# A graph network kernel on one core: four edits around edge preparation, the GCN projection and the first root's low parts

## The reference

```
L0  dense attention over an edge mask, 8 heads, then a feed-forward of 1024
L1  lin + PReLU, then twice: aggregate over edges, two 512x512 products, batch norm
L2  GCN: h = relu(layernorm(x)); aggregate(h / sqrt(deg)) @ W + b, leaky relu
L3  two relational layers: w[r] = sum_b att[r,b] * basis[b]   (30 bases of 512x512)
      out = x @ root + bias + sum_r A_r @ (gate_r * (x @ w[r]))
```

## Time and profile before

| | |
|---|---|
| median of 3 runs | 458.7 us (457.14 to 459.46) |
| profiled execution | 456.62 us, its span 454.8 us |
| TensorE busy | 438.6 us, 96% of the span |
| VectorE busy | 346.3 us, 76% |
| ScalarE busy | 243.7 us, 54% |
| GpSimd busy | 42.9 us, 9% |
| granted TensorE clock | 1.000 |
| DMA | 99.22 MB, mean 218 GB/s |

### The profile page before, as it was taken

The page is one execution under the profiler, slowest core; times in us unless marked ns, Lnnn a source line. Parts: engine busy times, 40 slices in busy tenths (PEclk is TensorE's granted clock), DMA queues, the critical chain, the costliest instruction groups (busy, mean ns, idle before and its releaser), DMA issues.

```text
span 454.8 us, 6200 instructions
## 1 busy us (share of the span) xinstructions
PE 438.6 (96%) x2226; PEld 274.3 (60%) x2226; DVE 346.3 (76%) x736; ACT 243.7 (54%) x428; POOL 42.9 (9%) x59
## 2 busy tenths in 40 slices
PE   8999999899997899999999999999998999999997
PEld 3334554443432346768776866677465788888885
DVE  5999996899999968688779657675759695866212
ACT  5999994676897617543345436544534623511210
POOL 3240000024223011000010000010000000000000
PEclk9999999999999999999999999999999999999999
DMA  7997347426699859978099766777973550000002
GB/s 254 415 398 176 110 174 308 179 93 219 235 380 353 295 206 332 409 272 345 11 372 404 295 246 251 275 252 267 375 199 115 225 186 1 1 0 2 0 3 92
DMA packets 18090, 99.22 MB, mean 218 GB/s; under 512 B 2959, under 2 KB 3599, under 8 KB 7567
## 3 DMA queue, kind: packets, MB, share of 16 engines
q1 hardware_dynamic: 13191, 72.72, 43.4%
q0 software_dynamic: 4000, 25.18, 15.1%
q10 hardware_dynamic: 864, 0.86, 0.6%
HBM read 93.50 MB, written 5.25 MB: 217 GB/s over the span
## 4 chain that ended last, share of the span: by engine, by line
PE 70%; DVE 12%; DMA 8%; issue 8%; ACT 1%; POOL 0%; DVEq 0%; POOLq 0%
PE bank L1371 15%; PE sbank L1703 10%; PE bank L1716 6%; PE sbank L1357 6%; PE sbank L1427 6%; PE bank L1608 5%; DMA bring<-in_basis 4%; PE bank L1688 4%; PE sbank L1567 3%; PE bank L1450 3%; DMA wring<-in_weights 3%; PE bank L1357 3%; PE bank L1513 2%; PE sbank L1337 2%; PE sbank L1490 2%
## 5 line engine op out<-in xcount | busy, mean ns | idle before, releaser
L839 DVE TENSOR_SCALAR cnt<-iota_row,edge_f 128x512 bf16<-128x512 f16 x132 | 41.4, 350 | 0.4 <-PE sbank L1427 0.4
L1357 PE MATMUL sbank<-bring,attw 120*32 120x512 f32 x336 | 41.0, 599 | 0.1
L1427 PE MATMUL sbank<-cnt,adjT 128*128 128x512 bf16 x132 | 30.6, 380 | 0.3
L466 ACT ACTIVATE stat<-stat,eps 128x1 f32<-128x1 f32 x32 | 9.4, 294 | 39.3 <-DVE stat L858 39.3
L576 ACT ACTIVATE adjT<-distance,edge_w,edge_f 128x128 bf16<-128x128 bf16 x61 | 29.2, 479 | 1.4 <-PE sbank L1427 1.4
L1281 DVE SCALAR_TENSOR_TENSOR y_lo<-sbank,gate,y_hi 128x512 fp32r<-128x512 f32 x16 | 11.8, 750 | 22.6 <-ACT y_hi L765 22.5
L497 ACT ACTIVATE s<-bank,colsb 128x512 f32<-128x512 f32 x24 | 16.4, 687 | 21.8 <-PE bank L1371 21.8
L1427 PEld LDWEIGHTS sbank<-cnt,adjT 128*128 128x128 bf16 x132 | 12.3, 98 | 21.7 <-DVE cnt L839 6.4
L529 ACT ACTIVATE distance<-iota_row,edge_f 128x128 bf16<-128x128 f16 x61 | 24.3, 400 | 1.8 <-DVE edge_f L905 0.4
L1371 PE MATMUL bank<-hT_hi,w_hi 128*128 128x512 f32 x64 | 25.3, 395 | 0.0
L1371 PE MATMUL bank<-hT_hi,w_lo 128*128 128x512 f32 x64 | 24.9, 390 | 0.0
(11 more groups left out here) (250 smaller groups left out, 1092.5 us busy)
## 6 DMA issues: line engine op xcount, KB each, us to landing
bring<-in_basis SPq DMA_DIRECT2D x59, 1024.0 KB, 9.8
wring<-in_weights POOLq DMA_DIRECT2D x8, 1024.0 KB, 10.0
landing<-in_weights POOLq DMA_DIRECT2D x4, 1024.0 KB, 5.1
w_scratch<-stage SPq DMA_DIRECT2D x16, 256.0 KB
hT<-in_weights POOLq DMA_DIRECT2D x4, 1024.0 KB, 9.1
qkw<-w_scratch POOLq DMA_DIRECT2D x2, 2048.0 KB, 7.9
rring<-in_rows POOLq DMA_DIRECT2D x12, 256.0 KB, 8.5
wring<-in_basis SPq DMA_DIRECT2D x2, 1024.0 KB, 12.9
```

The costliest lines, as they stand in the source:

```text
L839: dve.tensor_scalar(hot_s[:, n % HOT, :], iota[:, :], src_f[:, n:n + 1], None, ALU.is_equal).then_inc(sem("hot_ready"), 1)
L1357: mm = pe.matmul(unit_bank(b)[32 * j:32 * j + 32, :], attw[0:KB, u // UNITS, g, :], unit_place(u)[0:KB, j, :], start=(g == 0), stop=(g == ...
L1427: pe.matmul(bank[7][:, :], hot_d[:, n % HOT, :], hot_s[:, n % HOT, :], start=(n == 0), stop=(n == ECH - 1)).then_inc(sem("hot_used"), 1)
```

## The change

Five places are touched. (1) All four tiles of x are issued by SP; ACT's queue begins with `dst` and `src`, and `etype` counts on `cols_loaded`, which is now waited for at 48. (2) DVE prepares the destination's two parts, the source and the float of the destination ahead of the statistics of x; the relation, the field and the weight stay behind `hT0`. (3) The low parts of `root1` are written by POOL, behind its load and ahead of `load_w(0)`, and are gone from DVE. (4) `units(5)` and the four zero products become `units(6)`, so that every later unit of that stretch is one further on, and `units(2)` becomes `units(1)`. (5) The GCN projection runs in the order `BY_TILE`.

```
--- before.py
+++ after.py
@@ -318,7 +318,7 @@
             @block.sync
             def _(sp):
 
-                for c in (0, 2):
+                for c in range(C):
                     sp.dma_start(xr[:, c, :], x[:, c, :]).then_inc(sem(f"x{c}_loaded"), 16)
                 sp.dma_start(colsb[:, :], cols).then_inc(sem("cols_loaded"), 16)
                 sp.dma_start(alph[:, :], alphas.partition_broadcast(P)).then_inc(sem("cols_loaded"), 16)
@@ -402,6 +402,17 @@
                     pool.wait_ge(sem(last), C)
                     pool.dma_start(row(name), rows[i, :].partition_broadcast(P)).then_inc(
                         sem(f"row_slot{i % RSLOTS}_loaded"), 16)
+
+                def low_parts(name, ks=range(C)):
+
+                    hi, lo = weight_parts(name)
+                    i = IN_PARTS.index(name)
+                    for k in ks:
+                        pool.wait_ge(sem("weight_hi"), i * C + k + 1)
+                        if i and k == 0:
+                            pool.wait_ge(sem("weight_parts"), i * C)
+                        pool.tensor_tensor(lo[:, k, :], weight(name)[:, k, :], hi[:, k, :].bitcast(F32),
+                                           ALU.subtract).then_inc(sem("weight_parts"), 1)
 
                 def load_w(layer):
 
@@ -454,6 +465,7 @@
                     pool.dma_start(gate_rows[:, i, :], gate_scratch[i, :].partition_broadcast(P)).then_inc(
                         sem("gate_rows"), 16)
                 load_weight("root1")
+                low_parts("root1")
                 load_w(0)
                 load_weight("root2")
                 load_w(1)
@@ -531,10 +543,9 @@
 
 
                 my_chunks = [n for n in range(ECH) if on_act(n)]
-                for c in (1, 3):
-                    act.dma_start(xr[:, c, :], x[:, c, :]).then_inc(sem(f"x{c}_loaded"), 16)
-                for i, e in enumerate((src, dst, etype)):
+                for i, e in ((1, dst), (0, src)):
                     act.dma_start(edge_i[:, i, :], e).then_inc(sem("edges_loaded"), 16)
+                act.dma_start(edge_i[:, 2, :], etype).then_inc(sem("cols_loaded"), 16)
                 act.wait_ge(sem("small"), 1)
                 act.activation(root_of_eps[:, :], eps[:, :], ACT.Sqrt)
 
@@ -581,7 +592,7 @@
                     t, at = divmod(n - FIRST_TILE - TILE_LAG, TILE_EVERY)
                     if at == 0 and 0 <= t < 2 * C:
                         if t == 0:
-                            act.wait_ge(sem("cols_loaded"), 32)
+                            act.wait_ge(sem("cols_loaded"), 48)
                         qk_take(t)
                         if t == C + 1:
                             stage_units(BATCH)
@@ -874,6 +885,14 @@
                     dve.wait_ge(sem("v_psum"), c + 1)
                     dve.tensor_tensor(vr[:, c, :], bank[v_bank(c)][:, :], row("bv"), ALU.add).then_inc(sem("v"), 1)
 
+                dve.wait_ge(sem("edges_loaded"), 32)
+                dve.tensor_scalar(dst_part[:, 0, :], edge_i[:, 1, :], P - 1, None, ALU.bitwise_and).then_inc(
+                    sem("edge_step"), 1)
+                dve.tensor_scalar(dst_part[:, 1, :], edge_i[:, 1, :], P.bit_length() - 1, None,
+                                  ALU.logical_shift_right).then_inc(sem("edge_step"), 1)
+                dve.tensor_copy(src_f, edge_i[:, 0, :]).then_inc(sem("edge_step"), 1)
+                dve.wait_ge(sem("edge_step"), 3)
+                dve.tensor_copy(dst_lo, dst_part[:, 0, :]).then_inc(sem("edge_step"), 1)
                 for c in range(C):
                     dve.wait_ge(sem(f"x{c}_loaded"), 16)
                     norm_stats(0, xr[:, c, :], c)
@@ -887,15 +906,9 @@
                     dve.tensor_copy(hT[:, :, blk(P, c)],
                                     bank[c][:, :].rearrange("p (f n) -> p f n", f=C)).then_inc(sem("hT0"), 1)
 
-                dve.wait_ge(sem("edges_loaded"), 48)
-                dve.tensor_copy(src_f, edge_i[:, 0, :]).then_inc(sem("edge_step"), 1)
-                dve.tensor_scalar(dst_part[:, 0, :], edge_i[:, 1, :], P - 1, None, ALU.bitwise_and).then_inc(
-                    sem("edge_step"), 1)
-                dve.tensor_scalar(dst_part[:, 1, :], edge_i[:, 1, :], P.bit_length() - 1, None,
-                                  ALU.logical_shift_right).then_inc(sem("edge_step"), 1)
+                dve.wait_ge(sem("cols_loaded"), 48)
                 dve.tensor_scalar(rel1, edge_i[:, 2, :], 0.0, None, ALU.not_equal).then_inc(sem("edge_step"), 1)
-                dve.wait_ge(sem("edge_step"), 4)
-                dve.tensor_copy(dst_lo, dst_part[:, 0, :]).then_inc(sem("edge_step"), 1)
+                dve.wait_ge(sem("edge_step"), 5)
                 dve.scalar_tensor_tensor(field, rel1, float(C), dst_part[:, 1, :], ALU.mult, ALU.add).then_inc(
                     sem("edge_step"), 1)
                 dve.wait_ge(sem("edge_step"), 6)
@@ -916,7 +929,7 @@
                     if n == HOT // 2:
                         dve.wait_ge(sem("ident"), 2)
                         dve.tensor_scalar(never[:, :], ident[:, :], NEVER, None, ALU.mult).then_inc(sem("never_bq8"), 1)
-                        dve.wait_ge(sem("cols_loaded"), 32)
+                        dve.wait_ge(sem("cols_loaded"), 48)
                         dve.tensor_scalar(bq8[:, :], col("bq", 0, C), HD ** -0.5, None, ALU.mult).then_inc(
                             sem("never_bq8"), 1)
                     t, at = divmod(n - FIRST_TILE - TILE_LAG, TILE_EVERY)
@@ -1231,7 +1244,6 @@
                 split_weight("gcn")
                 for c in range(C):
                     T_lo("agg2", c)
-                split_weight("root1")
 
                 def xT_lo_part(layer, c):
                     dve.wait_ge(sem("xT_hi"), layer * C + c + 1)
@@ -1474,7 +1486,7 @@
                         if t:
                             units(2 if t == 2 * C - 1 else 1)
                 NH = N // 2
-                pe.wait_ge(sem("cols_loaded"), 32)
+                pe.wait_ge(sem("cols_loaded"), 48)
 
                 def products(it, pair):
 
@@ -1668,8 +1680,7 @@
                         mm = pe.transpose(bank[c][:, blk(P, f)], s1[:, f, blk(P, c)], ident[:, :])
                         if f == C - 1:
                             mm.then_inc(sem("x4_psum"), 1)
-                units(5)
-                keep_clock(4, bank[4])
+                units(6)
 
                 pe.wait_ge(sem("x5"), 2)
                 aggregate("h_gcn_parts", "agg2_psum", order=ALL_BANKS[:C], banks=AGG2_BANKS)
@@ -1677,7 +1688,7 @@
                 aggregate("h_gcn_parts", "agg2_psum", order=ALL_BANKS[C:], banks=AGG2_BANKS)
                 units(1)
                 pe.wait_ge(sem("x5"), C)
-                parts_stage("gcn", hT_parts, "agg2", "gcn_psum", t_major=False)
+                parts_stage("gcn", hT_parts, "agg2", "gcn_psum", order=BY_TILE, t_major=False)
 
                 def rel_root(layer, c):
 
@@ -1732,7 +1743,7 @@
                     turn(hr, c, ready, f"relT{layer}")
 
                 turn_rel(0, "h_rel0", 0)
-                units(2)
+                units(1)
                 turn_rel(0, "h_rel0", 1)
                 rel_root(0, 0)
                 turn_rel(0, "h_rel0", 2)
```

## The result

The changed kernel is slower: 461.38 us against 458.83 us (medians of 15 executions each), a ratio of 1.0054 with the interval 1.0035 to 1.0074, so +2.5 us where I forecast -0.3. The time lies inside the range that I gave, at its upper end.

What follows compares the result with a forecast made beforehand. TensorE was taken to set the end for 70%, with VectorE or loads holding it at two places. The GCN layer's -0.1 us and the start's -0.1, carried as -0.3 from 458.7, gave 458.4 us, range 455.6 to 461.4.

Steps and rivals of the forecast that it cites:

- The wait for unit 60: Ahead of the GCN aggregation: TensorE reaches unit 60 at 324.7 and waits 3.1 us for its load.
- drop its clock to the lower of the two levels: TensorE's wait before unit 60 halves its clock, 2.4 to 1.2 GHz, costing 2.7 us; chance 0.14.
- rival C: Slower: the wait before unit 60 lowers TensorE's clock, 2.7 us, giving 461.1 us; chance 0.14.
- the edges' transfers being small I take +0.5: At the start: statistics wait for two edge DMAs and move by +0.5 us, bounds 0 to +2.6.
- rival D: At the start: src lands near 6, statistics 2 us late, one-hots 1.5 us late, 459.9 us; chance 0.16.
- The nearest row: At the start: x0's load time of 3.75 us, applied to src, puts the statistics at 5.6, +1.1 us.
- The -0.55 us beside it: At the start: preparing edges earlier shortens the 1.55 us between hT's copies and the first one-hot by 0.55 us.
- The low parts on GpSimd: GCN layer: VectorE is freed of 2.50 us, GpSimd takes 4.8 us and holds VectorE 1.0 to 2.0 us.
- Where VectorE's advance went: GCN layer: VectorE's 2.4 us advance ends in a new wait, as the first turn stands behind the late projection.
- B's mechanism: Units 60 to 62 land some 2 us earlier, VectorE's 2.4 us come through, 455.7 us; chance 0.20.
- The sum: Whole kernel: -0.1 us at the GCN layer and -0.1 at the start, -0.2 together, rounded to -0.3: 458.4 us.
- A: The forecast itself: TensorE waits for the loads of units 60 to 62, 458.4 us; chance 0.50.

Runs made afterwards that it cites:

- clock kept: Changed kernel with the old start and 15 zero products ahead of unit 60, against the kernel before: 457.86 us, ratio 1.0006.
- start undone: Changed kernel with the old loads of x and the edges prepared in their old place, against the kernel before: 458.98 us, ratio 1.0031.
- start alone: Kernel before with only x loaded by SP and the edges prepared ahead of the statistics, against before: 459.78 us, ratio 1.0038.
- Low parts and tiles: Kernel before with only root1's low parts on GpSimd and the projection ordered by tiles, against before: 455.88 us, ratio 0.9958.
- `root1` loaded early: Kernel before with root1's low parts on GpSimd, projection by tiles and root1's load issued at c2_1, against before: 456.25 us, ratio 0.9969.
- low parts alone: Kernel before with only root1's low parts moved to GpSimd, projection in the old order, against before: 457.43 us, ratio 0.9994.

## Why the prediction was wrong

**The wait for unit 60: right.** 3.1 us forecast, 3.18 measured, with the landing 9.9 us after its issue (9.7 before). The issues did not move against the arrival, as I said. The landings moved a little: unit 61's came 9.4 and unit 62's 14.2 us after issue, where I took 9.9 and 15.5. TensorE, held up by its clock, shows no wait for either.

**"drop its clock to the lower of the two levels": the step that failed.** I saw the mechanism, sized it at 2.7 us, and then gave it a chance of 0.14, as a rival to the forecast; in the sum the clock stands at nothing. It is in the profiled execution after, and the mean clocks of all 15 (0.988 to 0.996) fit it, though a fall elsewhere lowers them too. Against the full-clock course (projection 19.5 us after arrival in the kernel with the clock kept, 19.3 forecast) it costs 2.2 us in the profiled execution after (21.74), 1.4 with the start undone (20.91). In the medians, start undone against clock kept, it is 1.1 us. My reason against it was that no row showed such a gap; that was a reason for an even chance, not a small one. My rival C has 461.1, 0.3 us from the measured 461.38, but that is luck: its 2.7 us were more than the clock took, and the start, which it left at -0.1, gave the rest. The Trainium skill (TensorE: Matmul & The Clock Gate, section "What's actually happening") has the clock at half rate after idling. The trace after agrees: 1.00 while TensorE was busy, 0.50 behind a wait of 3.18 us.

**"the edges' transfers being small I take +0.5": the second step that failed.** The statistics moved by 1.94 us, inside my bounds of 0 to +2.6, near rival D's 2. The nearest row gave +1.1, and I went below it on a guess; `src` took 4.6 us from issue to landing, where that row has 3.75. The -0.55 us beside it came true: statistics 1.73 us (start alone) and 1.94 us (after) late, first one-hots at 13.21 and 13.42, so 1.17 and 1.38 late; the counting then ends 1.0 and 1.2 us late. In the time it is +1.3 us at full clock; the rest of the 1.95 goes with executions in which the clock fell elsewhere, and stays open.

**The low parts on GpSimd: right in kind, low in size.** 4.8 us forecast, 5.49 to 5.95 measured; the holds of VectorE 1.64 us (0.67 and 0.97 over 0.69) against 1.0 to 2.0. One reading of mine was loose: the held operation of the softmax ended at 113.87 + 1.71 = 115.58, 1.08 us behind GpSimd's, and alone it takes 1.22, so a full block would have ended it at 115.7 and not at 115.5. By the rule of the Trainium skill on the shared ports (SBUF — State Buffer, section "SBUF: two separate sides") a hold could reach a whole GpSimd operation; the largest in the rows shown was 0.97 us, of operations of about 1.4 (5.49 by four); no run here shows a longer one, so the whole size was not put to the test. Both hidden, as forecast: VectorE held at tile 0 until 350.8, the turn stood behind the 48 matmuls until 354.91. The `qkw` load went out after the last tile of the projection, free of GpSimd's work.

**Where VectorE's advance went: right.** Low parts and tiles without the late units take 2.66 us off the stretch, and B's mechanism had 2.4: the edits make the path shorter, and the late projection takes it back, to +0.05 us with the clock kept. What I missed is that the whole of it needs both edits.

**The sum.** By the medians, taken to add up over three groups of executions, low parts and tiles are -1.95, the wait for the units +2.0, the clock +1.1, the start +1.95 by itself, +1.3 at full clock: together +2.5 to +3.1, and +2.5 was measured. The forecast had about -2.4, +2.4, 0 and -0.1. C and D happened together, which my chances had no place for; with both on top of A my own numbers give 458.4 + 2.7 + 1.5 = 462.6.

## What to carry to other kernels

Replace a filler that keeps TensorE busy by useful work only if this work's own load has landed by then; here it had not, and the wait came back (2.0 us) and the low clock with it (1.1 us). Two mishaps in different places can happen together: ask of rivals whether they exclude each other before giving out chances. And of edits made together try pairs as well as single ones: here the pair had the gain, and of the two kernels with one of them neither could be told from before.

## What the runs showed of the hardware

- The granted clock fell to 0.50 while TensorE was still waiting (0.93 in 328 to 330), and was back at 1.00 only between 336 and 339, with TensorE busy from 330.41 on. Matmuls of the aggregation were issued every 0.43 us there, every 0.23 us otherwise. With the start undone the clock was at 0.61 in 328 to 330, 0.53 in 330 to 332 and 1.00 from 332, so it was low for about half as long after a wait of the same kind; I have no row that says why. Nor is a wait of 3 us needed: around 149 us waits of 1.03 and 1.29 us left the clock at 1.00 in the profile of before, while 1.04 and 1.29, and 1.07 and 1.30, were followed by half clock in two other profiles (start alone, `root1` loaded early). So here the length of the waits alone doesn't say whether the clock falls.
- With the two 66 KB loads each at the head of its queue and x behind them, they landed in 2.1 and 2.3 us. At the head of ScalarE's queue, with all of x on SyncE's, `dst` took 3.8 us after, and `src`, second, 4.6.
- GpSimd and VectorE: the sum with x takes 1.66 us beside it in each of the three kernels shown, 0.69 alone; the operation before it took 1.53, 1.36 and 1.06 (low parts alone, after, low parts and tiles).
- Units 60 to 62, equal loads of 1 MB, landed 9.4 to 14.2 us after issue in one profile and 9.7 to 15.5 in another, and TensorE's arrival at the last units moved by up to 2 us between kernels that were the same ahead of it.
